# Scores and mixing of a graph attention kernel on 32x64 and 64x32 tiles of TensorE's array, without zero blocks in keys and probabilities

## What is computed

```
q = heads(x @ Wq + bq);  k = heads(x @ Wk + bk);  v = heads(x @ Wv + bv)
scores = einsum('bhqd,bhkd->bhqk', q, k) * scale
scores = where(mask[:, None] == 0, -inf, scores)
attn = softmax(scores, axis=-1)
out = einsum('bhqk,bhkd->bhqd', attn, v)
return layernorm(x + out @ Wo + bo)
```

## Time and profile before

| | us |
|---|---|
| median of 3 runs (lowest, highest) | 860.15 (859.45, 863.01) |
| the profiled execution | 857.66 |
| its span, first to last instruction | 855.9 |
| TensorE busy in it | 837.0 |
| VectorE, GpSimd, ScalarE busy | 540.7, 480.3, 284.5 |

### The profile page before, as it was taken

How to read it: one execution, slowest core, us unless ns; L and a number is a source line. 1 busy time by engine, 2 the same in 40 slices (tenths; PEclk the granted TensorE clock), 3 DMA queues, 4 the chain that set the end, 5 groups by cost and what they waited for, 6 DMA issues and landing times.

```text
span 855.9 us, 17597 instructions
## 1 busy us (share of the span) xinstructions
PE 837.0 (98%) x7177; PEld 686.9 (80%) x7177; DVE 540.7 (63%) x726; ACT 284.5 (33%) x401; POOL 480.3 (56%) x412
## 2 busy tenths in 40 slices
PE   8999999999999999999999999999999999999984
PEld 6878888888888888888888888888888888888863
DVE  4676557765557765567665567655577655676685
ACT  6543233342333332243332333423333322423210
POOL 3284557555466555566545575555665555654365
PEclk9999999999999999999999999999999999999998
DMA  8233353233433324333143432335323143321332
GB/s 323 70 92 126 100 153 94 62 112 88 154 99 88 107 61 155 100 111 116 53 130 100 147 97 51 126 88 154 100 88 105 63 155 99 105 75 50 112 96 90
DMA packets 50143, 91.86 MB, mean 107 GB/s; under 512 B 11280, under 2 KB 13328, under 8 KB 47888
## 3 DMA queue, kind: packets, MB, share of 16 engines
q1 hardware_dynamic: 37200, 72.91, 27.0%
q10 hardware_dynamic: 12864, 17.84, 7.6%
HBM read 40.37 MB, written 16.78 MB: 67 GB/s over the span
## 4 chain that ended last, share of the span: by engine, by line
PE 91%; DVE 4%; POOL 2%; issue 1%; DMA 1%; ACTq 1%; ACT 1%; POOLq 0%; DVEq 0%
PE ring L271 20%; PE ring L272 19%; PE ring L273 19%; PE psum_s L322 6%; PE ring L336 6%; PE ring L348 6%; PE ring L352 6%; PE ring L349 6%; DMA qt<-in_wq 1%; ACTq L501 1%; DVE soft L598 1%; POOL qt L183 0%; POOL row L183 0%; DVE top L606 0%; DVE total L610 0%
## 5 line engine op out<-in xcount | busy, mean ns | idle before, releaser
L632 DVE TENSOR_TENSOR row<-ring,row 128x512 f32<-128x512 f32 x60 | 41.5, 692 | 215.5 <-PE ring L352 215.5
L747 POOL TENSOR_TENSOR soft<-soft,top 128x1024 f32<-128x1024 f32 x62 | 118.9, 1918 | 78.6 <-DVE top L606 78.6
L176 POOL TENSOR_TENSOR soft<-soft,inverse 128x1024 f32<-128x1024 f32 x62 | 123.3, 1989 | 25.1 <-DVE inverse L613 22.1
L752 POOL TENSOR_TENSOR shifted<-moments,eps 128x1 f32<-128x1 f32 x64 | 12.1, 189 | 211.2 <-DVE moments L637 211.2
L481 ACT ACTIVATE kt<-ring,bk_slot,in_slot 128x512 f32<-128x512 f32 x128 | 92.4, 773 | 59.8 <-PE ring L273 59.8
L271 PE MATMUL ring<-wv_hi,x_hi 128*128 128x512 f32 x256 | 103.1, 403 | 0.0
L271 PE MATMUL ring<-x_hi,wq_hi 128*128 128x512 f32 x256 | 100.0, 391 | 2.0 <-DVE x_lo L648 2.0
L271 PE MATMUL ring<-x_hi,wk_hi 128*128 128x512 f32 x256 | 100.0, 391 | 0.8 <-ACT kt L481 0.8
L273 PE MATMUL ring<-wv_hi,x_lo 128*128 128x512 f32 x256 | 100.5, 392 | 0.0
L743 POOL TENSOR_TENSOR row<-row,bo 128x512 f32<-128x512 f32 x60 | 78.8, 1313 | 38.5 <-DMA row<-in_x 38.5
L272 PE MATMUL ring<-wv_lo,x_hi 128*128 128x512 f32 x256 | 100.4, 392 | 0.0
(11 more groups left out here) (77 smaller groups left out, 1484.3 us busy)
## 6 DMA issues: line engine op xcount, KB each, us to landing
pt<-soft SPq DMA_DIRECT2D x248, 64.0 KB, 2.3
pt<-soft ACTq DMA_DIRECT2D x248, 64.0 KB, 2.3
x_raw<-in_xt SPq DMA_DIRECT2D x15, 1024.0 KB, 6.8
row<-in_x SPq DMA_DIRECT2D x60, 256.0 KB, 3.2
out_rows<-row SPq DMA_DIRECT2D x60, 256.0 KB, 2.0
adj<-in_adj SPq DMA_DIRECT2D x16, 128.0 KB, 2.7
kt<-in_wk SPq DMA_DIRECT2D x4, 256.0 KB, 7.7
row<-in_wv SPq DMA_DIRECT2D x1, 1024.0 KB, 10.1
```

Source lines behind the costliest of these rows:

```text
L176: ops.tensor_tensor(soft_of(c), soft_of(c), on_keys(inverse[:, c % 2, :]), ALU.mult).then_inc(done, 1)
L747: nc.gpsimd.tensor_tensor(soft_of(c), soft_of(c), on_keys(top[:, c % 2, :]), ALU.subtract).then_inc(centred, 1)
```

## The change

Scores: one matmul per head and graph, with 32 rows of depth (the head's own features), 64 queries and 64 columns, on eight tiles of 32x64 of the array. kt holds each key once, without zeros. Mixing: one matmul per head and graph, with 64 rows of depth (the keys of that graph), 32 features and 64 columns, on eight tiles of 64x32; pt holds the blocks within a graph alone. Row tiles of the array that run at once have to write to different banks. So the scores of head r of each four go to bank r of psum_s, which now serves both tiles of a pair together, and mixing writes graph 0 of both tiles to one bank of the ring and graph 1 to the next. Since a bank now belongs to a pair, ScalarE's and VectorE's copies of ot go by pairs, 128x1024 at a time, and mask waits for the scores of both tiles. The products with zeros are gone.

```diff
-        kt = sb("kt", [P, 2, KC, 2 * GT, 2, NODES])
+        kt = sb("kt", [P, 2, KC, D])
-        pt = sb("pt", [P, 2, P // SQ, HEADS, SQ])
+        pt = sb("pt", [P, 2, 2, HEADS, SQ])
-        bias = sb("bias", [P, 2, GT, NODES])
+        bias = sb("bias", [P, 2, GT, 2, KC, SQ])
-        psum_s = ctx.enter_context(nc.psum_tensor("psum_s", [P, 2, 2, D], F32))
-        ring = [ctx.enter_context(nc.psum_tensor(f"ring{n}", [P, D], F32)) for n in range(4)]
+        psum_s = ctx.enter_context(nc.psum_tensor("psum_s", [P, HC, 2, 2, KC, SQ], F32))
+        ring = ctx.enter_context(nc.psum_tensor("ring", [P, 4, D], F32))
...
+        def ot_banks(p):
+            if p == FULL:
+                return s_banks(0, 2)
+            o = 2 if p > FULL else (p + 1) % 2 * 2
+            return ring[:, o:o + 2, :]
...
             def score(c):
-                wait_for(pe, masked, c - 1)
+                wait_for(pe, masked, c // 2 * 2)
...
                     for graph in range(2):
-                        rows = slice(t * P + graph * NODES, t * P + (graph + 1) * NODES)
-                        for pair in range(2):
-                            f = slice(pair * 2 * DH, (pair + 1) * 2 * DH)
-                            last = nc.tensor.matmul(
-                                psum_s[graph * NODES:(graph + 1) * NODES, c % 2, pair,
-                                       kc * 2 * NODES:(kc + 1) * 2 * NODES],
-                                qt[f, buf, kc, rows],
-                                kt[f, buf, kc, 2 * t + graph, :, :].rearrange("p s k -> p (s k)"),
-                                start=True, stop=True)
+                        own, rows = (slice(graph * NODES, (graph + 1) * NODES),
+                                     slice(t * P + graph * NODES, t * P + (graph + 1) * NODES))
+                        for r in range(HC):
+                            f = slice(r * DH, (r + 1) * DH)
+                            last = nc.tensor.matmul(psum_s[own, r, c % 2, :, kc, :], qt[f, buf, kc, rows],
+                                                    kt[f, buf, kc, rows].rearrange("p (b k) -> p b k", k=SQ),
+                                                    start=True, stop=True)
...
             def mix(c):
-                for h in range(HEADS):
-                    r, kc = h % HC, h // HC
-                    last = nc.tensor.matmul(ot_bank(c)[r * DH:(r + 1) * DH, kc * P:(kc + 1) * P],
-                                            v[:, c % 2, h * DH:(h + 1) * DH],
-                                            pt[:, c % 2, :, r // 2 * 2 * KC + kc * 2 + r % 2, :],
-                                            start=True, stop=True)
+                for kc in range(KC):
+                    to = slice((c % 2 * KC + kc) * NODES, (c % 2 * KC + kc + 1) * NODES)
+                    for r in range(HC):
+                        h = kc * HC + r
+                        for graph in range(2):
+                            own = slice(graph * NODES, (graph + 1) * NODES)
+                            last = nc.tensor.matmul(ot_banks(c // 2)[r * DH:(r + 1) * DH, graph, to],
+                                                    v[own, c % 2, h * DH:(h + 1) * DH], pt[own, c % 2, :, r * KC + kc, :],
+                                                    start=True, stop=True)
...
             def read_k(J):
-                for s in range(2):
-                    last = nc.scalar.activation(kt[:, buf, m, :, s, :], by_graph(k_bank(J)), ACT.Identity,
-                                                bias=bk_slot[:, s, m:m + 1], scale=in_slot[:, s:s + 1])
-                last.then_inc(k_done, 1)
+                nc.scalar.activation(kt[:, buf, m, :], k_bank(J), ACT.Identity,
+                                     bias=bk[:, m:m + 1], scale=1.0).then_inc(k_done, 1)
...
-            def read_ot(c):
-                act.wait_ge(mixed, c + 1)
-                wait_for(act, y_proj, c - 1)
-                nc.scalar.copy(ot_hi[:, c % 2].rearrange("p c q -> p (c q)"), ot_bank(c)).then_inc(ot_hi_done, 1)
+            def read_ot(p):
+                act.wait_ge(mixed, 2 * p + 2)
+                wait_for(act, y_proj, 2 * p)
+                nc.scalar.copy(by_chunk(ot_hi), mixed_rows(p)).then_inc(ot_hi_done, 1)
...
             def mask(c):
-                dve.wait_ge(scored, c + 1)
+                dve.wait_ge(scored, c // 2 * 2 + 2)
...
-            def split_ot(c):
-                dve.wait_ge(ot_hi_done, c + 1)
+            def split_ot(p):
+                dve.wait_ge(ot_hi_done, p + 1)
...
-            nc.gpsimd.memset(pt[:, :, :, :, :], 0.0).then_inc(const_done, 1)
```

More of the change, by code:

```diff
@@ L357, in _ @@
             for _ in range(WARM_START):
-                nc.tensor.matmul(ring[0][:, :], w_hi[3][:, 0, 0:P], w_hi[3][:, 0, :], start=True, stop=True)
+                nc.tensor.matmul(ring[:, 0, :], w_hi[3][:, 0, 0:P], w_hi[3][:, 0, :], start=True, stop=True)
             for kc in range(KC):
@@ L401, in _ @@
                 pe.wait_ge(v_done, a)
+                pe.wait_ge(k_done, a + 4)
                 mix(a - 2)
-                pe.wait_ge(k_done, a + 4)
                 mix(b - 2)
@@ L425, in _ @@
             pe.wait_ge(v_done, T - 4)
+            pe.wait_ge(k_done, T)
             mix(T - 6)
-            pe.wait_ge(k_done, T)
             mix(T - 5)
@@ L734, in make_bias @@
                 pool.sem_inc(pool_went_on, 1)
[L735 to L736 removed]
+                nc.gpsimd.tensor_scalar(
+                    bias[:, G % 2].rearrange("p t b c k -> p (t b) c k"),
+                    adj[:, :, :].rearrange("p t (b k) -> p (t b) k", k=SQ).unsqueeze(2)
+                    .to_broadcast([P, 2 * GT, KC, SQ]),
+                    0.0, MASKED, ALU.is_equal, ALU.mult).then_inc(bias_done, 1)
             def add_bo(c):
@@ L756, in make_rstd @@
                                         ALU.pow).then_inc(row_rstd, 1)
[L758 to L762 removed]
             nc.gpsimd.memset(eps[:, :], EPS)
[L764 to L765 removed]
+            nc.gpsimd.memset(minus_half[:, :], -0.5).then_inc(const_done, 1)
             pool.wait_ge(const_done, 1)
[L767 to L770 removed]
             make_bias(0)
```

102 lines of the change are left out of this document (35 added, 67 removed).

## The result

The changed kernel takes 909.8 us (median of 4 runs, 907.38 to 912.08), the kernel before 860.18 (859.45 to 863.01): a ratio of 1.0571, 95% interval 1.054 to 1.0602. The forecast was 866.6 us, with a range up to 892. The direction was right and the size far off. The profiled execution has a span of 909.3 us, at a mean granted clock of 0.973.

The account below looks back on a forecast made before the run. TensorE's stream was taken to bound the kernel: 855.9 - 47.9 (stages) + 52.8 (late pages) - 0.8 (head) + 2.3 (tail) = 862.3 us of span, 866.6 us as measured time, with a range up to 892.

Parts of the forecast that it names:

- head: Before the loop: TensorE's 0.8 us wait for ScalarE's copy of k would go, as it becomes one instruction: -0.8 us.
- Part 1, the array: Scores and mixing: eight tiles at once, 0.056 us a round, stages of 1.08 and 1.06 us; 47.9 us less.
- the last rival: Scores and mixing: the eight tiles don't overlap, so no gain per stage and pages still late; 887 us, chance 0.08.
- third rival: Scores and mixing: instructions handed out too slowly, no gain from 14 ns per record, 963 us at 27.3; chance 0.10.
- Part 2, the instructions: Scores and mixing: doubled instructions make TensorE wait for late 256-instruction pages, 1.94 us in most pairs; +52.8 us.
- F: Time from requesting an instruction page to its first instruction on TensorE: 3.2 us, each 0.1 us worth 3 us.
- The bound above: Upper limit of the page fetch time, from the longer packet at 531.11: 3.6 us, giving stalls of 65 us.
- Part 3, the merged copies: ot copied and split once per pair, mask and k copies merged: 0 in the loop, -0.8 us in the head.
- The new wait of project_q: In the loop, project_q(a + 4) waits for both tiles' split: 0.17 us, covered by stalls; without them 4.9 us in all.
- Part 4, the tail: After the loop: the merged split of T-4 and T-3 waits for ScalarE's copy and delays turn(T-1): +2.3 us.
- the sign: In the tail, what would show the forecast right: turn(T-1) starting 4.6 us later.
- The first rival: Scores and mixing: instructions arrive in time, no gaps, a period of 24.5 us; 818.7 us, chance 0.22.

Follow-up runs that it names:

- between_half_columns: The changed kernel with project_v between scores and mixing, each scores and mixing matmul reading only 32 of its 64 moving columns: 845.71 us.
- page_aligned: The changed kernel with semaphore increments making each pair exactly three instruction pages, plus 50 increments ahead of the loop: 845.75 us.
- page_misaligned: The same as page_aligned without the 50 increments ahead of the loop, so boundaries fall 73 and 329 instructions behind the scores' start: 903.22 us.
- between: The changed kernel with project_v(a) moved from behind the two mixing calls to between scores and mixing: 846.7 us.
- idle_gap: The changed kernel with project_v between scores and mixing and x loaded after mixing, plus a TensorE wait for two ScalarE copies per pair: 922.13 us.
- both_cures_tail: The changed kernel with project_v between, increments for three-page pairs, and in the tail ScalarE's copy of T-4 and T-3 ahead of T-2's issues: 867.61 us.

## Why the prediction was wrong, point by point

The sum missed the span by 47.0 us (862.3 against 909.3). By its own parts:

| term | forecast | measured | missed by |
|---|---|---|---|
| stages, 29 pairs (measured: with some 4 us of the long matmuls) | -47.9 | -24.7 | 23.2 |
| late pages | +52.8 | +62.3 | 9.5 |
| clock | none | +11.8 | 11.8 |
| other gap in the loop | none | +0.8 | 0.8 |
| head | -0.8 | +0.5 | 1.3 |
| tail | +2.3 | +2.7 | 0.4 |

The median is 0.5 above the span and not 4.3, which gives 3.8 back: 43.2 of the 43.2 us by which 866.6 was too low.

**Part 1, the array: the step that failed.** "Eight starts at 7 ns are 0.056 as well, so issue just keeps up." The round of eight in 0.056 us is there, in groups of eight, as forecast (8 records in 0.07 us), so the tiles do overlap and the last rival is out. But it holds for the first four rounds. I had taken the pace of a start (7 ns) for the pace of a stream; the 20 records in 0.55 us there come in rounds that the array sets, and the trace of before has no burst in which the array is faster than the hand-out. The forecast saw this case as its third rival and gave it a chance of 0.10, with an end at 27.3 ns and a threshold at 14. Measured over a whole stage it is 12.2 ns a record (1.56 us by 128), just below the threshold: of the 1.65 us per pair that were forecast, 0.70 stay. That rival was argued against by the four starts in 0.02 us behind a wait; between_half_columns shows that 32 records come at about that pace and no more. The range should have had a stage between 1.08 and 1.9 us in it, and not only in a rival. The rule of the Trainium skill, "TensorE: Matmul & The Clock Gate", section "Wait — 56ns, not 53.3ns?" (no start closer than 25 ns) would have made 3.2 us of a stage; as a mean over a stage, too, the trace has less than half of that between starts on different tiles.

**Part 2, the instructions: right in kind, too small, and by luck as near as it is.** Two pages of 256, 89 packets, the gap inside the stages, the end of the wait 1.2 to 1.6 us behind the packet: page_aligned against page_misaligned shows the page as the unit, and between undoes the loss. But the size came from two errors that partly cancel. A stage of 1.56 us instead of 1.08 hides more of a fetch: stepped through with the stages as measured, F = 3.2 us gives 37.6 us of gaps. The gaps of the changed kernel, 62.3 us, fit 4.0 to 4.1. The one fetch at 700 stood alone; in the changed kernel two or three pages follow each other, no two closer than 3.2 us, and in every second pair they stand behind the x load. The bound above, 3.6 us, was a packet's length, and it was too low because it left out the queue. The text said that F "will move with the other DMA traffic", and did not look up what traffic there is at the stages: the page of before lists that load.

**The clock: a term that was missing.** The sum put 50 us of idle time into TensorE's stream and kept its granted clock at 1.00 throughout. idle_gap shows that idle time by itself costs a second time: 16.4 us on top of 29 waits. In the changed kernel it is 11.8.

**Part 3, the merged copies.** The copy of k and the other engines' work cost nothing, as forecast. The new wait of project_q, kept for the case without stalls, is in no pair, not even in the one at 160.31: the stages there take 3.10 us and not 2.14, so project_q starts 8.68 us in, behind the split's end at 7.77. By the forecast's own figures, 7.84 against 7.71, that wait would have been 0.13 us and not 0.17. The head did not gain 0.8 us: TensorE's wait for that copy is still 0.8 us, as in the earlier trace rows.

**Part 4, the tail.** Forecast 2.3, measured 2.7, with some of it at half clock. VectorE waits 3.88 us for ScalarE's copy ahead of its split at 885.04, and turn(T-1) starts 5.1 us later behind the loop's end than before, for the 4.6 given as the sign. both_cures_tail, where the tail is 3.0 us shorter without the blocked copy, agrees with the cause.

**The first rival** (instructions in time, 818.7) had the wrong price too: with no late page the loop takes 25.2 us a pair, not 24.5, and the kernel 844 and not 819.

## What to carry to other kernels

Count instructions as a resource of TensorE's stream. Here 256 of them took some 3.2 to 4 us to arrive, and behind the first 64 of a burst they were handed out at about 6 ns each, whether a record read 32 columns or 64. Smaller tiles with more instructions paid here only where long matmuls stood between the bursts, or where the page boundaries fell in the right places. So look for work to put between bursts before giving such a change up: one move of 12 matmuls was worth 63 us and turned a loss of 6% into a gain of 1.6%. And when a sum adds idle time to TensorE, price what its clock may lose behind it as well.

## What the runs showed of the hardware

- Instruction pages of TensorE are fetched one after the other: no two packets start less than 3.2 us apart in any trace here (the packet itself is 0.9 to 1.6 us in the changed kernel and up to 2.2 in others), and behind a late page TensorE goes on 1.2 to 1.6 us after the packet's end, but for two gaps in first pairs (0.9 and 2.3).
- They are late behind other DMA traffic: with the engines at 0.95 to 1.01 share a packet began 1.8 us behind its boundary, and with the x load moved the gaps fell from 62.3 to 52.2 us.
- A semaphore increment in TensorE's program takes 0.15 us: 50 in one place take 7.6 us, of which 2.6 showed as lost time; spread between long matmuls, 55 per pair cost nothing that can be seen (undisturbed periods of 24.95 to 25.1 us, 25.09 in the changed kernel).
- A stage of 128 records takes 1.44 (mixing) to 1.59 us (scores) with 64 columns on eight tiles and 1.29 to 1.49 with 32, medians of the undisturbed ones.
- Gaps of about 2 us, behind a late page or behind a wait for another engine, are followed in some pairs by 3.4 us at a granted clock of 0.50.
